# Reordered opening, a later head division, later second rows and unpaced weight loads in a two-layer cross-attention and expert kernel

## The reference

```python
# layer 0
x = x + attention0(layernorm(x), ctx)                  # Wq, Wk, Wv, Wo with biases
x = x + top1_experts0(layernorm(x))                    # 8 experts, 256 -> 512 -> 256, gelu
# layer 1
x = x + attention1(layernorm(x), ctx)                  # normalised q, k, v
h = layernorm(x)
x = x + shared(h) + sum over 2 of 7 routed experts     # silu(h @ g.T) * (h @ u.T) @ d, 256 -> 704 -> 256
```

## Time and profile before

| what | value |
| --- | --- |
| median of 3 runs | 514.07 us |
| lowest and highest | 508.97 and 516.68 us |
| the profiled execution | 516.68 us |
| its span | 515.4 us |
| TensorE busy | 495.7 us (96%) |
| VectorE busy | 259.0 us (50%) |
| ScalarE busy | 201.0 us (39%) |
| GpSimd busy | 87.6 us (17%) |

### The profile page before, as it was taken

The page is one execution under the profiler, slowest core; times in us unless marked ns, Lnnn a source line. Parts: engine busy times, 40 slices in busy tenths (PEclk is TensorE's granted clock), DMA queues, the critical chain, the costliest instruction groups (busy, mean ns, idle before and its releaser), DMA issues.

```text
span 515.4 us, 8828 instructions
## 1 busy us (share of the span) xinstructions
PE 495.7 (96%) x3293; PEld 370.9 (72%) x3293; DVE 259.0 (50%) x776; ACT 201.0 (39%) x416; POOL 87.6 (17%) x124
## 2 busy tenths in 40 slices
PE   7899999999999999999999999999999999999994
PEld 6555555658998887654555356656999998999993
DVE  4778897764374754976648653512322222222220
ACT  3647555452646445446245641311222222222221
POOL 2447000004020200200000000470022121121122
PEclk9999999999999999999869999999999999999998
DMA  8820009995132300480000030296886676686622
GB/s 290 247 66 1 2 26 346 368 349 170 42 104 63 104 31 22 126 283 2 1 0 2 1 122 1 56 319 202 288 260 201 205 256 190 214 263 193 211 22 27
DMA packets 43383, 73.13 MB, mean 142 GB/s; under 512 B 3553, under 2 KB 33729, under 8 KB 43332
## 3 DMA queue, kind: packets, MB, share of 16 engines
q1 hardware_dynamic: 34580, 60.47, 35.4%
q0 software_dynamic: 4336, 6.75, 6.0%
q10 hardware_dynamic: 4416, 5.26, 3.2%
HBM read 56.35 MB, written 14.51 MB: 137 GB/s over the span
## 4 chain that ended last, share of the span: by engine, by line
PE 73%; DVE 13%; DMA 8%; issue 2%; ACT 2%; POOL 1%; ACTq 0%; SPq 0%; POOLq 0%; DVEq 0%
PE PS L2009 15%; PE PS L892 9%; PE PS L2024 8%; PE PS L1918 7%; PE PS L902 6%; PE PS L923 4%; PE PS L1929 4%; PE PS L1791 4%; PE PS L1804 3%; DVE W L1095 3%; DMA VR<-scratch_rows 3%; PE PS L402 3%; PE PS L376 2%; DMA out<-PR,slots 2%; PE PS L911 2%
## 5 line engine op out<-in xcount | busy, mean ns | idle before, releaser
L1095 DVE TENSOR_REDUCE W<-PS 128x2 f32<-128x512 f32 x128 | 83.8, 686 | 41.1 <-PE PS L892 40.2
L2009 PE MATMUL PS<-PR,W 128*128 128x128 f32 x836 | 96.5, 275 | 0.0
L2009 PEld LDWEIGHTS PS<-PR,W 128*128 128x128 f32 x836 | 94.9, 192 | 0.1
L892 PE MATMUL PS<-W 32*128 32x256 f32 x512 | 85.7, 411 | 3.1 <-DVE W L1095 1.8
L902 PE MATMUL PS<-W 32*128 32x512 f32 x256 | 79.8, 654 | 0.2
L892 PEld LDWEIGHTS PS<-W 32*128 32x128 f32 x512 | 56.8, 190 | 26.7 <-issue 12.0
L2024 PE MATMUL PS<-W,PR 128*128 x228 | 52.5, 380 | 0.8 <-ACT PR L2742 0.8
L2793 POOL DMA_INDIRECT out<-PR,slots x19 | 29.7, 1563 | 135.3 <-ACT PR L2742 131.7
L1262 ACT ACTIVATE PR<-PS 128x512 f32<-128x512 f32 x64 | 35.2, 595 | 35.5 <-PE PS L902 35.4
L2024 PEld LDWEIGHTS PS<-W,PR 128*128 128x128 f32 x228 | 41.9, 190 | 6.1 <-issue 1.2
L2045 DVE TENSOR_TENSOR PR<-PR,PS 128x512 f32<-128x512 f32 x19 | 13.1, 688 | 59.7 <-PE PS L2009 59.7
(11 more groups left out here) (274 smaller groups left out, 620.2 us busy)
## 6 DMA issues: line engine op xcount, KB each, us to landing
W<-in_rguT SPq DMA_DIRECT2D x19, 1408.0 KB, 6.2
W<-in_L_ffn_W SPq DMA_DIRECT2D x16, 512.0 KB, 9.7
W<-in_rdT SPq DMA_DIRECT2D x5, 768.0 KB, 9.8
scratch_rows<-W SPq DMA_DIRECT2D x1, 2860.0 KB, 14.9
VR<-scratch_rows SPq DMA_DIRECT2D x19, 130.0 KB, 5.5
W<-in_mask SPq DMA_DIRECT2D x2, 1024.0 KB, 13.7
scratch_x<-W SPq DMA_DIRECT2D x1, 2048.0 KB, 15.2
PR<-scratch_x SPq DMA_DIRECT2D x16, 128.0 KB, 2.3
```

The source lines that it names most:

```text
L892: m = pe.matmul(PS[:, bank, q * FK:(q + 1) * FK], QT[r:r + 32, g, c:c + 128], KT[r:r + 32, g, b * FK:(b + 1) * FK], start=True, stop=True)
L1095: dve.tensor_reduce(NM[:, s % 2, q:q + 2, c], PS[:, m_bank(use), :].rearrange("p (q n) -> p q n", q=2), AX, ALU.max).then_inc(sem("m_free" ...
L2009: m = pe.matmul(PS[:, bank, j * 128:(j + 1) * 128], W[:, o:o + 128], XS[:, r % 2, k, :], start=(k == 0), stop=(k == 1))
```

## The change

1. DMA order. SP: the weights of V in the place of `ct_1`, the first half of mask 0 ahead of x tiles 4 to 7. ACT: x tiles 2 and 3 ahead of `cols`, `ct_1` and the second half of the mask ahead of the weights of Q.
2. ScalarE runs `keys_compact(0)` ahead of the normalised rows. TensorE groups the values in pairs, both of the first pair behind the turn. VectorE runs the `cb` operations, mask half 0, the copy of `XT`, mask half 1, and only then the statistics of x tiles 4 to 7.
3. The division of group 6 in layer 1 goes from ahead of `shared_dve` into `beside1(0)`, behind product 0.
4. The turn of the second rows goes from chunk 2 to 3, the logits from 3 to 4, the ranks, gates, places and tables into chunk 5.
5. The first three `load_up` go together, without the wait for product 7 and ahead of the rows.

```diff
     def sp_start():
         load_keys0(sp, 0)
         sp.dma_start(X[:, 0:2, :], x_v[:, 0:2, :]).then_inc(sem("x0"), 16)
-        load_keys0(sp, 1)
+        sp.dma_start(WP[:, 1, :, :], A["L0_xattn_WvT"].rearrange("(k p) n -> p k n", p=128)).then_inc(sem("wp_1"), 16)
+        load_mask0(sp, 0)
         sp.dma_start(X[:, 4:8, :], x_v[:, 4:8, :]).then_inc(sem("x1"), 16)
-        load_mask0(sp, 0)
...
     def act_start():
+        act.dma_start(X[:, 2:4, :], x_v[:, 2:4, :]).then_inc(sem("x0"), 16)
         act.dma_start(cols[:, :, :], A["cols"]).then_inc(sem("col"), 16)
-        act.dma_start(X[:, 2:4, :], x_v[:, 2:4, :]).then_inc(sem("x0"), 16)
-        act.dma_start(WP[:, 1, :, :], A["L0_xattn_WvT"].rearrange("(k p) n -> p k n", p=128)).then_inc(sem("wp_1"), 16)
+        load_keys0(act, 1)
+        load_mask0(act, 1)
         act.dma_start(WP[:, 2, :, :], A["L0_xattn_WqT"].rearrange("(k p) n -> p k n", p=128)).then_inc(sem("wp_2"), 16)
-        load_mask0(act, 1)
...
+        keys_compact(0)
         act.wait_ge(sem("stats"), NORMS[True]["x0_0"])
         for i in (2, 3):
             normal_act("x0_0", i, XN[:, i, :], X[:, i, :]).then_inc(sem("xn"), 1)
-        for f in range(2):
-            keys_compact(f)
+        keys_compact(1)
...
-        pe.wait_ge(*at(0, "wp_1", 16))
-        values_of(0)
...
             turn4(2 + k, [XN[:, j, :] for j in range(4)], k).then_inc(sem("turned"), 1)
-        values_of(1)
+        pe.wait_ge(*at(0, "wp_1", 16))
+        values_pair(0)
...
         projected_T(0, 2, 0, XT[:, :, 0:512]).then_inc(sem("q_ps"), 1)
-        values_of(2)
...
         projected_T(1, 2, 1, XT[:, :, 0:512]).then_inc(sem("q_ps"), 1)
-        values_of(3)
+        values_pair(2)
...
-        dve.wait_ge(sem("x1"), 16)
...
-        dve.wait_ge(*at(0, "turned", 2))
-        dve.tensor_copy(XT[:, 1, 0:512], PS[:, 3, :]).then_inc(sem("xt"), 1)
-        mask0_ones(0)
         dve.wait_ge(sem("col"), 16)
...
+        mask0_ones(0)
+        dve.wait_ge(*at(0, "turned", 2))
+        dve.tensor_copy(XT[:, 1, 0:512], PS[:, 3, :]).then_inc(sem("xt"), 1)
         mask0_ones(1)
+        dve.wait_ge(sem("x1"), 16)
+        for t in range(4):
+            dve.bn_stats(ST[:, COLUMN["x0_1"] + t, :], X[:, 4 + t, :]).then_inc(*v.up())
...
# second_pe, beside1
-            elif n == 2:
+            elif n == 3:
                 pe.wait_ge(*at(1, "rows", 8))
                 turn_batch("rows1_1", rows_for(1, 1))
-            elif n == 3:
+            elif n == 4:
                 taken(6, "rows1_1")
                 claim(7, "logits1_1")
                 filled(7, logits_pe(1, 4, 4, 7))
-            elif n == 4:
+            elif n == 5:
                 claim(7, "ranks1")
                 filled(7, ranks_pe(2))
...
# second_dve, beside1 
             if n == 0:
+                dve_divide(1, 6, v)
                 dve_divide(1, 7, v)
...
-            elif n == 2:
+            elif n == 3:
                 dve_xt("rows1_1", 1)
-            elif n == 3:
+            elif n == 4:
...
-            elif n == 4:
+            elif n == 5:
                 gates1(v)
                 dve.wait_ge(*full(7, "ranks1"))
                 whole(places1(v, full_free(7, "ranks1")))
-            elif n == 5:
                 whole(tables1(v))
-        dve_divide(1, 6, v)
         shared_dve(beside1)
...
# sp_way
-            load_up(0)
-            sp.wait_ge(sem("mul"), CHUNKS - 4)
-            load_up(1)
+            for r in range(UPS):
+                load_up(r)
             sp.wait_ge(sem("scattered"), SCATTERED[2])
             load_x(0)
             load_x(1)
-            load_up(2)
```

More of the change, by code:

```diff
@@ L733, in keys_half, with values_pair @@
             return m
[L735 to L738, removed]
+        def values_pair(j0):
+            for j in (j0, j0 + 1):
+                m = projected(4 + j // 2, j, 1, CTf, KCOLS[j])
+            m.then_inc(sem("vals_ps"), 1)
         pe.wait_ge(sem("consts"), 2)
@@ L806, in dve_start @@
         dve.tensor_scalar(cb[:, 0, :], cols[:, C_COMPACT, :], 0.25, None, ALU.mult).then_inc(sem("col_bias"), 1)
+        mask0_ones(0)
+        dve.wait_ge(*at(0, "turned", 2))
+        dve.tensor_copy(XT[:, 1, 0:512], PS[:, 3, :]).then_inc(sem("xt"), 1)
         mask0_ones(1)
+        dve.wait_ge(sem("x1"), 16)
+        for t in range(4):
+            dve.bn_stats(ST[:, COLUMN["x0_1"] + t, :], X[:, 4 + t, :]).then_inc(*v.up())
+        dve.wait_ge(*v.now())
+        for t in range(COLUMN["x0_1"], COLUMN["x0_1"] + 4):
+            dve.bn_aggr(MV[:, t, :], ST[:, t, :]).then_inc(sem("aggregated"), 1)
         values(0)
```

## The result

| what | before | after |
| --- | --- | --- |
| median | 511.48 us (20 runs) | 514.20 us (20 runs) |
| lowest and highest | 508.97 and 516.68 | 513.20 and 517.53 |
| profiled execution, its span | 516.68, 515.4 | 517.48, 516.2 |
| ratio, 95% interval | | 1.0068, 1.0054 to 1.0083 |

The change makes the kernel slower by 0.7%, some 3.5 us (0.0068 x 511.5), and the interval is clear of 1. That is less than the 2% from which a change counts as slower, so it counts as the same. The forecast was +3.65, counted from 514.07, the median of the first three runs. With twenty the kernel before has 511.48; most of the 3.5 by which 517.7 lies above 514.20 is that starting point.

The account below looks back on a forecast made before the run. TensorE, busy 495.7 of 515.4 us, was taken as the bound. Terms 0 + 1.65 + 1.6 + 0.4 = 3.65 us on a 514.07 median gave 517.7 us, own range 515 to 520.5, wider range 511.0 to 523.5.

Parts of the forecast that it names:

- The opening: Opening, 0 to 25 us: gains and costs of the new orders cancel, 0 us, bounds -1 and +3.
- Point (a): Opening: x rows 2 and 3 load one issue earlier, landing about 7.1, turn forward by 0.5 us at most.
- Point (b): Opening: ct_1 goes later, batch 1 keys begin about 10.1; normalised rows shift -0.4 to +0.4 us, taken as 0.
- Point (d): Opening: x0_1 statistics go behind both mask conversions; GpSimd's chain starts later but shrinks 2.2 to 4.4 us, cost 0.
- The division: Start of shared experts: TensorE's turn of outputs 7 waits for group 6's division, +1.65 us, bounds +1.3 and +2.0.
- The wait before down(6): Shared experts: TensorE waits for VectorE's places, tables and additions, +1.6 us, bounds 0.8 and 2.5.
- Rows of tile 0: Start of routed experts: scatter 9.3 us later uses up 8 us of slack, +0.4 us, bounds 0 and 3.2.
- Chunk 8 finds its product ready, so no more: Shared experts after down(6): no further TensorE wait was expected in later chunks.
- R1: Not slower: the opening brings scores 1 us forward and stalls reach lower bounds, 514 us; chance 0.1.
- R2: Half-clock stretch near 251 to 266 us lost (510.7) or a second one drawn (524.7); chance 0.2.
- R3: Weight-load burst holds back the scatter's packets, rows late: 525.6 us, or 522.5 without slow opening; chance 0.12.
- R4: Shared experts: the two stalls aren't there, their waits being satisfied earlier, 514.5 us; chance 0.08.

Follow-up runs that it names:

- v_opening: Kernel before with x tiles 2 and 3 second on ACT, ct_1 left on SP, V weights behind cols, new mask loads and engine orders; ratio 1.0020, median 510.95 us.
- s_half: Changed kernel with the second half of the scatter left out (8 indirect DMAs instead of 16); ratio 1.0105, median 515.7 us.
- e4_opening: Kernel before with only the opening's new DMA order and new engine orders; ratio 1.0008, median 511.78 us.
- e1_divide: Kernel before with only the division of group 6 moved behind product 0; ratio 1.0020, median 512.7 us.
- e2_chunks: Kernel before with only second rows, logits, ranks, gates, places and tables moved to later chunks; ratio 1.0072, median 515.2 us.
- w_34: Kernel before with the later division of group 6 and the later rows, logits and ranks, nothing else; ratio 1.0104.
- u_divide: Changed kernel with the division of group 6 put back ahead of the shared experts; ratio 1.0102, median 516.35 us.
- u_hold: Changed kernel with the first three weight loads put behind the loads of routed rows; ratio 1.0272, median 524.8 us.
- u_paced: Changed kernel with paced weight loads again: second behind product 7, third behind the rows; ratio 1.0117, median 517.04 us.
- e3_burst: Kernel before with only the first three weight loads issued together; ratio 0.9999, median 511.56 us.
- s_late: Changed kernel with GpSimd beginning its scatter only after product 9 of the shared experts; ratio 1.0380.
- p_45: Kernel before with the later rows, logits and ranks and the three weight loads together, nothing else; ratio 1.0073, median 515.18 us.

## Why the prediction was right, and where it was not

**The opening, predicted 0.** It measured +0.64 in the profile of after. Point (a) came: x landed 0.5 earlier. Point (b) is the term that was mis-sized: ct_1 took 8.76 us, issue to landing, where the weights of V in that place had taken 7.7, so it came at 11.15 and not at 10.1. In v_opening the weights of V, in that place again but behind the new order, took 8.8 themselves, so the length belongs to the order of the loads and not to ct_1. The four key products then took 1.15 where the working had 0.9. As a bound I had named that a new pause between the batches of keys might put off the faster pace. It was late in a part of the executions. The chain of waits in s_half's opening:

```profile
2.39 8.55 DMA CT<-in_ctxT
10.94 0.04 issue
10.98 2.09 PE PS L731 x4
13.07 0.02 issue
13.10 0.69 ACT W L693
13.78 0.99 ACT PR L473 x2
14.77 0.14 issue
14.91 1.94 PE PS L376 x8
```

ct_1 is even 0.2 earlier, yet the same key products take 2.09 instead of 1.15, and the turn 1.94 instead of 1.06. The second turn of the changed opening came at 25.0 to 25.1 in three traces, at 25.9 to 26.7 in four; with the old one at 24.4 to 25.1 in five and 26.2 in one. On the mean 25.8 against 24.9, so 0.8 (before rounding). e4_opening's median, +0.4 with bounds of -0.9 and +1.7, is compatible with that and with 0. Point (d) held: both conversions were over before GpSimd began, its chain was 4.5 long, and turn_second didn't wait for it. Here the Trainium skill's rule ("SBUF — State Buffer", the shared port pair) was needed and the trace bears it out once more: an operation on 128x4 took 1.31 beside VectorE's conversion and at most 0.27 without one. The record of that operation begins 0.06 us ahead of the conversion's (14.88 and 14.94), so which of the two came second can't be read from it.

**The division, predicted +1.65.** In the trace 1.57 of waiting, and 0.63 for a turn that took 0.44: +1.73 by place. Right, and in every trace that has the edit. The time gives less: with the edit and without it in three pairs (before and e1_divide, e2_chunks and w_34, u_divide and the change) the ratio moved by +0.002, +0.003 and -0.003. Weighted by their intervals that is +0.5 us, with bounds of -0.7 and +1.7. Much of that noise is the clock. For each execution the mean granted clock is known, and span times clock is an estimate of the span at the upper level. By it e1_divide is 1.9 us above the kernel before, with bounds of 1.0 and 2.8, which bears the forecast out.

**The wait before down(6), predicted +1.6.** +1.2: 0.96 of waiting and 0.24 for products that run longer behind a stop. Posi, tables and additions came as reckoned, each a little sooner.

**Rows of tile 0, predicted +0.4.** 0. The scatter began 36.2 behind the turn of outputs 7 instead of 29.0. The forecast's 9.3 later holds the 1.5 of standing before that turn; counted behind the turn it has 36.7 (337.6 less 300.93), and for the loads of rows 58.2, which measured 57.9. So the chain was reckoned 0.5 and 0.3 too long, and rows landed in 2.1, the short end. TensorE itself was later by the next wait, which alone would have hidden the 0.4.

**What I had not seen: down(10).** 1.9 of waiting and 1.5 of lower clock in this profile. The prediction's step that had no such term was "Chunk 8 finds its product ready, so no more". All seven traces with edit 4 and the whole scatter at its usual place have the wait (1.2 to 2.0), none of the five without edit 4 has it. Edit 4 doesn't make it by its own work: it moves the scatter by 7.2 us against the chunks. At one issue in 1.27 us, thirteen of the sixteen scatters are issued when the silu of chunk 10 is due. In the twelve traces with the whole scatter at its usual place a silu is due with thirteen or fourteen issued, and in eleven it was late. Due, begun, landing of the scatter: the change 349.4, 355.1, 354.0; u_hold 349.4, 354.9, 353.7; w_34 351.0, 356.6, 355.4; e1_divide 344.0, 348.7, 347.9. So ScalarE stood 4.7 to 5.7 us and went on about 1 behind the landing (in e2_chunks and u_paced 4.1 us, and 0.3 ahead of the landing). The twelfth is the kernel before, with the scatter landed at 349.8 and fourteen issued:

```profile
346.16 0.60 ACT L1948 ACTIVATE PR<-PS 128x512 f32<-128x512 f32 x1 [4.56 <-PE PS L1918]
```

With ten issued it was mixed (e3_burst due 335.7, begun 339.9; v_opening 1.5 late; e1_divide on time at 338.84); with fewer, all were on time within 0.3, s_late (six) and s_half (eight at the most) among them. A silu of chunks 6 to 9 may be nearly 5 us late at no cost to TensorE, as e1_divide shows, which has no wait from that. It is no rule: in e3_burst, where VectorE stood as well, TensorE waited 2.4 before down(8). Chunk 10 has less, since the up of chunk 11 is half as long, and edit 4 moves the last third of the scatter upon it.

What ScalarE lacks there isn't settled. Shown: no wait before down(10) without the late part of a scatter beside it (s_half, s_late), and the wait is there without weight loads in the queues (u_hold). The Trainium skill ("Runtime: NRT & Kernel Launch", Instruction fetch mechanics) says that engines fetch their instructions in blocks by DMA, mostly hidden. A held block would have fitted, but the change's trace has one instruction packet between 325 and 358 us, and that at 356, when the silu had begun. It doesn't support this.

**The sum.** By the profiles: 0.6 + 1.7 + 1.2 + 0 + 3.4 for down(10) with its clock - 0.6 for shorter waits of the routed part (148.3 instead of 148.9 us) = 6.3. The spans differ by 0.8 only, since the kernel before lost 6.8 at half clock; the 1.3 that is left lies between the second turn and the first chunk. That stretch took 271.3 us before (264.5 without the half clock) and 265.7 after, and in the other traces 263.3 to 266.2 with their clock taken off, so it belongs to single executions.

The median has +3.5. So a part of the 6.3 is not in every execution. The profiled one was among the slowest of its kernel (517.48; highest 517.53). With those that ran beside the experiments there are 46 executions of the change. By span times clock 31 of them lie from 508.6 to 511.3 and 15 from 511.9 to 513.7, the profiled one (513.6) with these; the kernel before has 507.2 in the mean of 71. A late silu in the one group and not in the other would look like that. That is argued, not shown: only one of them has a trace. The two stalls that the prediction named are borne out; that their sum with the rest came so near the 3.5 is partly luck, since a cost of 1.9 or more that I had not seen met others that count less in the median than in the trace.

**Rivals.** R1 (514, the opening pays) fell with the traces: the opening cost. R2: the stretch near 251 is absent from all the other profiles, with the change or without. But seven of them (the four parts alone, u_divide, w_34, p_45) have a shorter one between 220 and 235 us, in u_divide at 0.76 and 0.56 over 10 us, which cost it 3.4. The change, u_hold, u_paced, s_half, s_late and v_opening have none. So each part occurs with such a stretch; whether the whole change keeps it away isn't settled. R3 fell. The issues kept their places in e3_burst and in the change. Its packets do stand behind the weights, but they did so before as well. The DMA queues of the change from 336 to 340 us (packets, MB, share of the engines; q1 carries the weights, q0 the scatter):

```profile
q1 hardware_dynamic: 192, 1.08, 93.1%
```

and from 340 to 344:

```profile
q1 hardware_dynamic: 221, 1.15, 69.4%
q0 software_dynamic: 181, 0.53, 32.7%
```

and of the kernel before from 333 to 337:

```profile
q1 hardware_dynamic: 174, 0.98, 92.0%
```

In both, for 4 us the weights run and the scatter moves nothing, though GpSimd goes on issuing. In the change it catches up before its end: the last issue ends at 352.3, the landing is at 354.0. So it cost the rows nothing. With half as many scatters it has no time to: in s_half the last issue ends at 343.1 and the landing is at 348.2. R4 is refuted by the waits.

**What edit 5 is worth.** From u_paced to the change 0.0049 less, from e2_chunks to p_45 0.0001 more (without edit 4, from the kernel before to e3_burst, 0.0001 less). The first two together make -0.9 us, with bounds of -2.2 and +0.5: not settled, though the waits for rows shrank both times (1.7 to 0.6, 1.9 to 0.4). No version tried was measured faster than the kernel before.

## What to carry to other kernels

Where one engine is busy 96% of the span and is itself the chain, moving another engine's work has little to gain: look in the chain for each place that will now wait for the moved piece, and add up those waits. Then follow what the move delays downstream (here the scatter), and ask of everything that shares its last microseconds how much slack it has; the piece with the least (the half chunk at the end) decides. A later load for an early product can cost more than its delay, if TensorE is slower behind the pause that it makes: four of the seven traces with the new opening had their second turn 0.8 to 1.7 us behind the other three. And the mean granted clock of each execution is worth a look where times scatter by more than the effect.

## What was not expected of the hardware

- With ten or more of GpSimd's sixteen indirect DMAs issued and the last not yet landed, ScalarE can stand with its input ready: 4.7 to 5.7 us in the four traces listed above, at a DMA share of 0.29 as well as at a full one. VectorE did so once, for 3.7 us (e3_burst). The cause is open.
- While the first weight loads of SP ran, no packet of GpSimd's scatter moved for 4 us, in the kernel before and in the change, though its issues went on; from 340 to 344 in the change both moved.
- Four key products took 1.15 us behind a pause that ended at 11.20 and 2.09 behind one that ended at 10.98, and the turn behind them 1.06 and 1.94: the pace after a stop differs from execution to execution of the same opening.
- A wait of 1.9 us of TensorE near 355 was followed by 3 us at granted clock 0.50 in the change's trace and by 2 us at 0.54 and 3 at 0.74 in that of p_45 (1.9), and by none at all in those of u_divide (2.0) and w_34 (1.8).
